# The end of a fused router, decay-attention and router kernel: the last output product moved ahead of the second block's router product, two mixes on other banks, one block's statistics taken apart into earlier steps

## The reference

```python
x = x + 0.5 * ffn(layernorm(x))
x = x + attn(layernorm(x))
x = x + 0.5 * ffn(layernorm(x))

# ffn, for each token:
logits = flat @ router_weight.T + router_bias        # 64 experts
scores = softmax(logits)
topk_w, topk_idx = top_k(scores, 8)
w_dense = the eight weights in their places, 0 elsewhere
out = flat * topk_w.sum() + w_dense @ expert_bias

# attn, end of it:
y = y_intra + y_inter                                # per head and chunk
y = y / rms(y) * gnorm_w * silu(hidden @ Wg.T)
out = y @ Wo.T                                       # summed over all heads
```

## Time and profile before

| | us |
|---|---|
| median of three runs | 1631.44 |
| lowest, highest | 1631.27, 1636.41 |
| profiled execution, whole | 1634.31 |
| its span in the profile | 1632.5 |
| PE busy | 1587.2 (97%) |
| POOL busy | 1412.8 (87%) |
| DVE busy | 1368.7 (84%) |
| ACT busy | 1093.5 (67%) |

### The profile page before, as it was taken

The page is one execution under the profiler, slowest core; times in us unless marked ns, Lnnn a source line. Parts: engine busy times, 40 slices in busy tenths (PEclk is TensorE's granted clock), DMA queues, the critical chain, the costliest instruction groups (busy, mean ns, idle before and its releaser), DMA issues.

```text
span 1632.5 us, 33589 instructions
## 1 busy us (share of the span) xinstructions
PE 1587.2 (97%) x11028; PEld 885.4 (54%) x11028; DVE 1368.7 (84%) x2945; ACT 1093.5 (67%) x2987; POOL 1412.8 (87%) x1316
## 2 busy tenths in 40 slices
PE   7898999999999999999999999999999999999986
PEld 6554555555555555555555555555555555555554
DVE  7988788888879888797879888887888878788976
ACT  5666676676766667766766667666676767676653
POOL 5777899888988999888988999888998989888964
PEclk8999999999999999999999999999999999999998
DMA  6022233232343224231532223222332224222222
GB/s 223 28 56 67 59 74 85 65 73 53 79 85 78 53 59 107 50 85 46 92 83 62 63 66 87 72 72 53 86 84 59 72 46 105 65 65 58 48 46 104
DMA packets 208012, 118.76 MB, mean 73 GB/s; under 512 B 173792, under 2 KB 174816, under 8 KB 206816
## 3 DMA queue, kind: packets, MB, share of 16 engines
q1 hardware_dynamic: 207840, 116.63, 30.0%
HBM read 70.19 MB, written 4.46 MB: 46 GB/s over the span
## 4 chain that ended last, share of the span: by engine, by line
PE 74%; POOL 13%; DVE 7%; issue 4%; ACT 2%; ACTq 0%; POOLq 0%; DVEq 0%
PE B L323 24%; PE B L325 23%; PE B L324 23%; POOL ROWS L1428 2%; POOL QS L1415 2%; POOL RR L1461 2%; POOL PL L1450 1%; POOL WVL L1446 1%; DVE WL L1701 1%; POOL ZS L1454 1%; POOL RM L1458 1%; POOL WVF L1438 1%; POOL K L1422 1%; PE B L553 1%; DVE PF L1645 1%
## 5 line engine op out<-in xcount | busy, mean ns | idle before, releaser
L323 PE MATMUL B<-WH,XTH 128*128 128x128 bf16 (+1 forms) x992 | 270.0, 297 | 5.0 <-DVE VL L1630 4.3
L324 PE MATMUL B<-WL,XTH 128*128 128x128 bf16 (+1 forms) x992 | 269.8, 297 | 0.0
L325 PE MATMUL B<-WH,XTL 128*128 128x128 bf16 (+1 forms) x992 | 269.8, 297 | 0.0
L1415 POOL TENSOR_TENSOR QS<-QS,SIN 128x512 f32<-128x512 f32 x160 | 219.5, 1372 | 33.6 <-ACT QS L1142 33.0
L323 PE MATMUL B<-XTH,WH 128*128 128x512 bf16 x640 | 243.3, 380 | 1.1 <-DVE G L1635 1.1
L325 PE MATMUL B<-XTH,WL 128*128 128x512 bf16 x640 | 243.3, 380 | 0.0
L324 PE MATMUL B<-XTL,WH 128*128 128x512 bf16 x640 | 243.1, 380 | 0.0
L1694 DVE SCALAR_TENSOR_TENSOR YF<-B,RR,G 128x128 f32<-128x128 f32 x512 | 144.1, 344 | 113.4 <-POOL RR L1461 113.3
L1174 ACT ACTIVATE PF<-ROWS,NG 128x128 f32<-128x128 f32 x512 | 162.8, 390 | 79.3 <-POOL ROWS L1428 78.9
L1454 POOL TENSOR_TENSOR ZS<-YF,ZS 128x512 bf16<-128x512 f32 x128 | 158.0, 1235 | 64.4 <-ACT ZS L1212 64.2
L1428 POOL TENSOR_TENSOR ROWS<-ROWS,AFTER 128x512 f32<-128x512 f32 x128 | 190.1, 1485 | 2.5 <-DMA ROWS<-rows_dram 2.5
(11 more groups left out here) (209 smaller groups left out, 4319.8 us busy)
## 6 DMA issues: line engine op xcount, KB each, us to landing
ROWS<-rows_dram SPq DMA_DIRECT2D x128, 256.0 KB, 3.2
STAGE<-in_wall SPq DMA_DIRECT2D x108, 256.0 KB, 2.8
ACC<-in_x SPq DMA_DIRECT2D x3, 1024.0 KB, 9.1
out<-ACC SPq DMA_DIRECT2D x3, 1024.0 KB, 3.9
ZT<-ZS SPq DMA_TRANSPOSE x128, 3.1
ACC<-in_x SPq DMA_DIRECT2D x4, 256.0 KB, 3.7
COS<-in_cos SPq DMA_DIRECT2D x1, 1024.0 KB, 12.8
SIN<-in_sin SPq DMA_DIRECT2D x1, 1024.0 KB, 14.8
```

Source lines behind the costliest of these rows:

```text
L323: nc.tensor.matmul(out_, ah, bh, start=first, stop=False)
L324: nc.tensor.matmul(out_, ah, bl, start=False, stop=False)
L325: return nc.tensor.matmul(out_, al, bh, start=False, stop=last)
L1415: nc.gpsimd.tensor_tensor(QS[:, sl, :], QS[:, sl, :], SIN[:, t0:t0 + TB], ALU.mult).then_inc(sin_ready.sem, 1)
```

## The change

Four edits, all in the last head and behind it:

- In `mix`, the third and fourth mix of the first block go to B2 and B6, which until then hold the transposes of the second block, and no longer to B1 and B3. Their waits change with it: for ACT's copies of those transposes (`f_xnt`) and not for the additions of chunks 13 and 14. `pe_turn` of the third block, which uses B2 and B6 next, now waits for the additions of those mixes. In the second block the third and fourth mix, on B1 and B3, wait for the additions of chunks 14 and 15.
- On PE the product of chunk 15 stands ahead of the router product of the second block, without the wait for `f_acc`.
- On DVE the addition of chunk 15 stands right behind the first block's four additions and no longer behind `dve_weigh(NB + 1)`.
- The third block's statistics (four BN_STATS, four BN_AGGR) leave their place behind the first block's additions: two BN_STATS go into step 13, one into step 14, one and the BN_AGGR into step 15, each ahead of `gated` (in step 15 ahead of `dve_logits(NB)` too).

```diff
-            return BANK[(4, 5)[i % 2] if f < NB else (5, 4, 1, 3)[i]]
+            return BANK[(4, 5)[i % 2] if f < NB else (5, 4, 2, 6)[i] if f == NB else (5, 4, 1, 3)[i]]
...
+                if f == NB + 2 and i < 2:
+                    pe.wait_ge(f_acc.sem, acc_at(NB, i + 2))
...
                 if f == NB and i >= 2:
-                    pe.wait_ge(out_free.sem, out_free.at(KVH - 1, (NCH - 2, NCH - 3)[i - 2]))
-                elif f == NB + 1 and i == BLK - 1:
-                    pe.wait_ge(out_free.sem, out_free.at(KVH - 1, NCH - 1))
+                    pe.wait_ge(f_xnt.sem, f_xnt.at(NB + 1, i))
+                elif f == NB + 1 and i >= 2:
+                    pe.wait_ge(out_free.sem, out_free.at(KVH - 1, NCH - 4 + i))
...
             pe_mix(pe, NB)
+            project_out(KVH - 1, NCH - 1, True)
             pe_logits(pe, NB + 1)
-            pe.wait_ge(f_acc.sem, acc_at(NB, BLK - 1))
-            project_out(KVH - 1, NCH - 1, True)
             pe_turn(pe, NB + 2)
...
+                if last and n >= NCH - 3:
+                    dve_stats(dve, 0, NB + 2, ((0, 1), (2,), (3,))[n - NCH + 3])
...
             dve_mixed(dve, NB)
-            dve_stats(dve, 0, NB + 2)
+            add_out(KVH - 1, NCH - 1, True)
             dve_logits(dve, NB + 1)
             dve_choose(dve, NB + 1)
             dve_weigh(dve, NB + 1)
-            add_out(KVH - 1, NCH - 1, True)
             dve_stats(dve, 0, NB + 3)
```

## The result

| | us |
|---|---|
| kernel before, median of ten runs made beside the changed kernel's | 1633.49 (1631.27 to 1636.41) |
| changed kernel, median of ten runs | 1639.9 (1635.29 to 1643.79) |
| ratio, with its 95% interval | 1.003 (1.002 to 1.004) |
| the same as a difference | + 4.9 (+ 3.3 to + 6.5) |
| changed kernel, profiled execution: whole, span | 1635.62, 1633.4 |

By the ratio the changed kernel is slower by 4.9 us; the forecast was + 4.2. (The two medians lie 6.4 apart, which is still inside the interval, up to + 6.5.) The median lies above the range on record (up to 1638.4), but that range stood on a median of three runs, 1631.44, and the larger sample of the same kernel came out at 1633.49. Laid on 1631.44, the ratio gives 1636.3, which is inside.

A forecast was written before the change was run, and what follows sets the result against it. PE was taken as the bound, meeting DVE at the second block's logits. A 2.68 us shift there plus 1.5 from a low clock made + 4.2, forecast 1635.6 us, range 1631.9 to 1638.4.

The forecast's parts named there:

- Steps 13 and 14: BN_STATS put ahead of the gates on DVE, two in step 13, one in step 14: cost nothing.
- Step 15: One BN_STATS and four BN_AGGR ahead of the gate on DVE: gate and first mix 0.79 us later, bounds 0.6 and 1.0.
- The mixes: First block's eight mixes on PE: end 0.34 us later, or 0.79 if the low clock stretch moves with them.
- The first case: Low clock stretch on the first block's mixes stays in place: they end only 0.34 us later.
- The product ahead: Chunk 15's product ahead of the second block's router product on PE: 2.59 us, less 0.26 by which PE was early.
- DVE's 2.80: Statistics time saved on DVE behind the first block's additions: all 2.80 us goes into two waits for PE.
- The new gap: PE idles 3.0 us ahead of the third block's second pair of transposes, waiting for ACT.
- The clock: Low clock behind PE's new gap, on the third block's transposes and router product: 1.5 us lost, bounds 0 and 1.7.
- The second rival: Both ends high plus one more low clock stretch in the last blocks: + 6.5 us, 1637.9; chance 0.13.
- It passes to the end: From PE's router product of the third block on, work is as before, so the 4.2 us shift reaches the end.
- Three: Later third and fourth blocks remove the low clock stretch at 1618.2: + 2.5 us, or + 1.0 without the new fall; chance 0.12.
- Four: DVE, not PE, bounds behind the additions, so the second block's logits start sooner: - 1.4 us, 1630.0; chance 0.04.

The follow-up runs named there:

- e4: Changed kernel with the fourth BN_STATS and the four BN_AGGR moved from step 15 to behind the first block's additions; 1638.4 us, ratio 1.0024.
- e11: e7 with the fourth BN_STATS and four BN_AGGR moved from step 15 to ahead of the second block's logits; 1632.32 us, ratio 0.9995.
- e9: The changed kernel itself, same code, profiled a second time; that execution took 1640.5 us.
- e1: Changed kernel with the product of chunk 15 and its addition back in their old places; 1634.72 us, ratio 1.0009.
- e3: Kernel before with only the third block's statistics moved into steps 13 to 15; 1636.77 us, ratio 1.0012.
- e7: e1 with unused products added, eleven ahead of the first block's turned weights and twelve ahead of the third block's mixes; 1634.44 us, ratio 0.9988.
- e12: Changed kernel with unused products in three PE gaps: first block's weights, third block's transposes, third block's mixes; 1634.18 us, ratio 1.0006.
- e2: Changed kernel with the third block's statistics put back behind the first block's additions, behind the addition of chunk 15; 1638.77 us, ratio 1.0029.
- e10: The changed kernel itself, same code, profiled a third time; that execution took 1640.68 us.
- e6: Kernel before with twelve unused products added on PE ahead of the third block's mixes; 1635.46 us, ratio 0.9998.
- e5: Changed kernel with twelve unused products added on PE between the third block's two pairs of transposes; 1638.79 us, ratio 1.0017.

## Why the prediction was right, and where its size was off

**The total.** By the ratio + 4.9 (+ 3.3 to + 6.5) against + 4.2, and by the path that was forecast. That the two numbers lie so close is in part luck: the three profiles of the changed kernel have + 2.5, + 7.8 and + 7.9 in the tail, none of them near 4.2, and it is their mixture, with a sum that starts 1.6 to 2.0 sooner, that comes out near it.

**Steps 13 and 14, no cost.** Right. The sum of step 15 comes no later behind that of step 12 (25.75 to 25.85 in every profile), and in e4 and e11, which have these statistics, gate and first mix stand at 3.28 or 3.27 and 9.24, against 3.27 and 9.24.

**Step 15, 0.79 later.** The mechanism was right, the size was 0.53 for the gate, 0.54 for the first mix (0.75 where the clock had already fallen on the turning of the weights, as in e9). 1.00 was added; of it 0.47 was covered and not the 0.21 that stood as the wait ahead of the addition. Before, the addition began 0.39 behind the start of the instruction ahead of it (1583.92 to 1584.31) and the gate 0.75 behind that; in the changed kernel it is 0.08 (1583.31 to 1583.39) and 0.60 (to 1583.99). A recorded wait was here not the whole of what an instruction behind it could hide.

**The mixes, 0.34 or 0.79.** The first case has the right mechanism where the low stretch is as before: in e1 and e3 it stayed, the mixes begin 0.56 and 0.59 later, and the router product behind them only 0.22 and 0.21. (Six products at 0.42 and two at 0.22 from 1591.82 end at 1594.78, so that case should have read 0.42.) In the changed kernel it is neither case. The low stretch did not stay where it was: in the first profile it was not there at all and the eight products took 1.74 (1589.97 to 1591.71); in e9 it covered all eight mixes and much of the product behind.

**The product ahead, 2.59, less 0.26.** Right, and e7 against e12 gives the 2.59 to the hundredth.

**DVE's 2.80 go into two waits.** Right: 0.94 and 2.83 in the first profile, in e1 and e3 one of 2.47.

**The new gap, 3.0 us.** Right: 2.96 in the first profile, 2.95 in e2 and e9, 2.96 in e4, each ended by ACT's copy.

**The clock, 1.5 (0 to 1.7).** This is the term that was mis-sized. In the first profile it came out at + 1.51 and in e2 at + 1.57. In e4, e9 and e10 it is 3.27 to 4.02 up to the third block's logits and 0.77 to 1.15 more up to the fourth's. The failing step is "3.4 us of gapless work at half rate lose 1.7": it took the length of the low stretch from the two before, where bfloat16 products of 512 columns followed the gap. Behind the new gap follow float32 transposes and the router product of 64 columns, and the clock stayed at 0.50 through 10.1 us of them. The kind of work does not decide it alone: in the first profile the same instructions had the clock back after about 3 us, and in e9 the low stretch of 6.8 us lay on bfloat16 products. In the same way 1.04 more were lost on the product of chunk 15 in e9. The second rival, 6.5, at a chance of 0.13, comes nearest to the 7.8 of e9 in size. Its mechanism was another: it had one low stretch more in the last blocks, and e9 has two longer ones (6.8 and 10.2 us) and one fewer there.

**It passes to the end.** Nearly: 2.77 at the fourth block's logits became 2.50 at the end of the first profile, 8.57 became 7.81 in e9 (where 6.6 was left at DVE's last addition).

**Rivals three and four.** Three was half right: in e9 and e10 the low stretch on the third block's mixes is indeed gone. But it is worth little at the end, as e6 shows, which takes it away outright: 1.49 at DVE's last addition, 0.27 at the end, not 1.7. Four fell: the statistics' departure alone (e1, e3) moved the logits by 0.05 and 0.06.

The prediction had weighed that the window over which the activity is judged runs freely, so that a gap of one length may or may not bring a fall (the Trainium skill, TensorE: Matmul & The Clock Gate, Part 1). By that rule one kernel should show several outcomes, and the traces agree: in the changed kernel's profiles the first block's mixes ran once at 1.00 and twice at 0.50 to 0.52. But in all three the new gap of 3 us was followed by a fall. What varied there was the length of the low stretch, about 3 us or 10.1, so the error was to let the uncertainty reach down only, to 0, and not up.

**What stays open.** Why e3's median is 2.7 above before while its profiled tail is equal. Its gate comes 0.53 later, as in the changed kernel, so PE's wait ahead of the first block's weights is longer, and it may be that its executions too have the long low stretch there now and then. Six of e3's twelve executions and three of e1's eleven lie above 1637.2, and of the 84 of the kernel before that were made beside the experiments one does; so the statistics in step 15 may cost something that no profile here caught. No profile shows e3 so; this is argued only. What decides between a short and a long low stretch was not settled either. And the sum's own start, 1579.8 to 1583.8, varies by up to 4 us, made in the first 120 us, where the low stretches too stand in different places (the kernel before has one at 99.3 us, the first profile of the changed kernel one at 62.2). That is as much as the effect and is why ratios of whole executions tell so little between e7, e11 and the kernel before. Why it comes sooner in the six profiles named above is open.

## What to carry to other kernels

Before moving a block of matrix work forward on PE, look at what it filled where it stood: here twelve products had kept PE's wait for ACT at 0.64 us, and moved away they cost their own 2.59 us once on the path and left a gap of 3 us that lowered the clock for whatever came next. Taking work off an engine gains only as long as the other side of the meeting point isn't due at the same moment; 0.26 us of slack was all there was for 2.80 us saved. And where the clock is a term, profile the kernel more than once: the first profile showed + 2.5 in the tail, the two others + 7.8 and + 7.9.

## What the hardware showed that was not expected

- The granted clock can stay at 0.50 through work without a gap: PE was busy 10.10 of 10.10 us (e9) and 10.20 of 10.20 (e4), on transposes and on the float32 router product of 64 columns. In the first profile of the same kernel it was back at 0.96 about 3 us after the gap.
- A gap of one length need not bring a fall. PE's wait of 2.65 us ahead of the third block's mixes in e9 was followed by 1.00, that of 3.10 before by 0.50; the wait ahead of the first block's weights was 2.75 in both the first profile of the changed kernel and e9, and the mixes ran at 1.00 in the one and at half rate in the other.
- Eleven or twelve unused products of 512 columns in such a gap held the clock at 1.00 in each of the places where they were tried: ahead of the first block's weights (e7, e11, e12; of the eleven profiles without them nine have a low stretch on the mixes), between the third block's transposes (e5, e12; without them five of five fell), ahead of the third block's mixes (e6, e7, e11, e12; without them eight of ten fell). Between e9 and e5 they removed 3.3 us of loss; in e6 they were worth 1.49 us at DVE's last addition and 0.27 at the end.
- One BN_STATS and four BN_AGGR, 1.00 us of DVE's work, moved the gate behind them by 0.53 us.
